# A graph layer on one core: GpSimd hands one of 64 row gathers to SyncE

## The chip, the cores and the metric

The kernel runs on 1 core of one Trainium2 chip. The metric is the device time of one execution in microseconds (us), as the median of several runs. The engines are TensorE (PE; its weight loads are shown apart, as PEld), VectorE (DVE), ScalarE (ACT), GpSimd (POOL) and SyncE (SP). Rows with a q (SPq, ACTq, DVEq) are work of an engine's own queue of instructions: waits, register work, the issue of transfers.

## The reference

One layer of message passing over N = 12500 nodes of 64 values and E = 200000 edges. `src` is random; `dst` is sorted and denser at low nodes. In short:

```
nodes   = x[[src, dst]]                        # E x 128
gates   = (ssp(edge_attr @ We1 + be1) @ We2 + be2) * cutoff(edge_weight)
h       = ssp(nodes @ Wn1 + bn1) @ Wn2 + bn2   # ssp(v) = softplus(v) - ln 2
sums    = zeros_like(x).at[dst].add(h * gates)
new     = x + ssp(sums @ Ws1 + bs1) @ Ws2 + bs2
return layernorm(x + new)
```

## The kernel before

The edges are taken in 391 **quads** of 512, in order of `dst`. A quad has two pairs of 256 edges; a pair's destinations lie in one range of W = 64 nodes, whose first node is in the table `w_all`. SP and DVE read it into registers (TENSOR_LOAD in the trace, L378 for SP and L1140 for DVE). For each quad:

- **POOL** (its `fast_step`) gathers the rows `x[src]` into `ga`, four indirect DMAs of 128 rows each (L459), into a ring of ARING = 16 quads. Before a quad it waits until PE has transposed the quad 15 earlier (`xe_t`).
- **SP** (its `fast_step`, one turn for two quads) reads four range starts (L378), waits on `oht_b` for DVE's pick of three quads before (L325), then issues `relb` (L326, the edges' places in their ranges), four `bw` (L335, one range's rows each of the table `b_tab`, which is x times the lower half of Wn1) and one `ea` (L318, the edge attributes of two quads). `ea` and `relb` have rings of 4 quads, `bw` one of 8. Between turns it stores shares of `b_tab` (L357) in the first quads, and finished nodes (L399) from quad 221 on, every 8 quads.
- **PE** in step s: `front(s)` (L623, L585) makes both hidden layers' inputs, where the second half of L623 multiplies `bw` by DVE's one-hot `ohT`; `transposes(s+2)` (L575 for `ea`, L577 for `ga`); `back(s-3)` (L653) sums messages over their ranges; `mid(s-1)` (L636, L640) is the second layers. `transposes` waits for `ea` and `ga` to have landed.
- **ACT** in step s: absolute values of `front(s)` (L852, L854), copy of the transposes (L844), exp (L860), a fill of PSUM with the bias (L871), log (L865).
- **DVE** in step s: `hidden(s-1)` (L1114, L1118), `message(s-2)`, `pick(s+2)` (L1100, `ohT` from `relb`), `one_hot(s-1)` (L1106), and `flush(s-3)` (L1152), which adds a range's sums to `acc` at an address from a register.

From step 206 on, every 8 steps one group of 500 nodes is finished beside the edges (L662, L671 on PE); three groups are left for the end. In steps 4 to 95 the shares of `b_tab` are made in the same way. Steps are written out or looped on each engine by hand; nothing plans them. There is a general path for other data; a flag chooses at run time and this data take the fast one. With sorted edges a pair's destinations must lie within W nodes for that.

Of the kernel before, what the change touches and what calls it, by code (L numbers as in the profile page):

```python
# [9 lines left out]
I32 = mybir.dt.int32  # L10
# [5 lines left out]
P = 128  # L16
PAIR = 2 * P
QUAD = 2 * PAIR
W = 64
# [5 lines left out]
BRING = 8  # L25
IN_RANGE = "windows' places are the least of N - W and of destinations, which are nodes"

# [29 lines left out]
def gnn_layer(nc, x, src, dst, edge_attr, dist, We1, be1, We2, be2, Wn1, bn1, Wn2, bn2,  # L57
# [29 lines left out]


# [20 lines left out]
    with ExitStack() as ctx:  # L109
# [10 lines left out]
        w_tab = nc.dram_tensor("w_tab", (1, RG * P * 2), I32, kind="Internal").ap()  # L120

# [63 lines left out]
        bw = sb("bw", [P, BRING, F])  # L185
        relb = sb("relb", [P, RING, PAIR], U8)
# [14 lines left out]
        dst_i = rows_d[:, :, :].rearrange("p g e -> p (g e)")[:, 0:NT].bitcast(I32)  # L201
        gen_flat = sb("gen_flat", [P, 10 * P])
# [58 lines left out]

        filled, hg_set = sem("filled"), sem("hg_set")
# [21 lines left out]
        def _(sp):  # L284
# [22 lines left out]
            def load_ea(q, u):  # L307

                if reached(q, RING):
                    sp.wait_ge(xe_t, q - (RING - 2))  # L310
                if isinstance(q, int) and q == NQ - 1:
                    full = edge_attr[q * QUAD:q * QUAD + PAIR, :].rearrange("(p j) d -> p (j d)", j=2)
                    sp.dma_start(ea[:, u, 0, :], full).then_inc(s_ea[u], 16)
                    part = edge_attr[q * QUAD + PAIR:E, :].rearrange("(p j) d -> p (j d)", j=2)
                    sp.dma_start(ea[0:REMP // 2, u, 1, :], part).then_inc(s_ea[u], 16)
                else:
                    two = edge_attr[bass.ds(q * QUAD, 2 * QUAD), :]
                    sp.dma_start(ea[:, u:u + 2, :, :].rearrange("p q k c -> p (q k) c"),  # L318
                                 two.rearrange("(m p j) d -> p m (j d)", p=P, j=2)).then_inc(s_ea[u], 16)

            def load_rel(q, u):

                if reached(q, RING):
# [1042 lines left out]
```

## Time and profile before

| what | value |
|---|---|
| median of 3 runs | 1991.15 us (1990.34 to 1991.43) |
| the profiled execution | 1991.78 us, of which the span of the profile is 1989.6 us |
| mean granted TensorE clock | 0.946 of full speed |
| busy, of the span | PE 88%, POOL 75%, ACT 74%, DVE 64% |
| chain that ended last | POOL 55%, "issue" 20%, PE 14% |
| DMA | 157.78 MB, 79 GB/s over the span |

How to read it: busy time is the time in which an engine had an instruction in it; "issue" is time in which an engine waited for nothing that the profile shows. The chain is followed back from the last instruction, at each step to what released it. Releasers are inferred. The profile covers one execution, and its durations are of that one.

### The profile page before, as it was taken

The page shows a single profiled execution, that of the slowest core. Times are in us where ns is not written, and L with a number is a line of the kernel's source. Part 1 is how long each engine was busy: PE and PEld are TensorE (multiplying, and loading weights), DVE is VectorE, ACT ScalarE, POOL GpSimd, SP SyncE. Part 2 cuts the span into 40 slices and gives each one's busy share as a digit, 9 for nine tenths or more (in the row PEclk, how much of TensorE's full clock was granted, in tenths as well). Part 3 has the DMA queues.
Part 4 walks back from the last instruction along what each step waited for, and adds up shares of the span by engine and source line. Part 5 has one row for each costly group of instructions (what it writes and reads, how often), then busy time and mean ns, then how long its engine had stood idle before and what let it go on. Part 6 is the DMA issues. An engine that isn't in the chain of part 4 may idle for free.

```text
span 1989.6 us, 52758 instructions
## 1 busy us (share of the span) xinstructions
PE 1744.9 (88%) x16249; PEld 1331.2 (67%) x16249; DVE 1281.8 (64%) x3512; ACT 1470.9 (74%) x2586; POOL 1483.8 (75%) x1572
## 2 busy tenths in 40 slices
PE   4699999989889888899888998888998898888897
PEld 3477777777667666666666776666776666666666
DVE  4577777766655655656566666666666666666666
ACT  2478888877776777767677777777777777777776
POOL 7777777777777777777777777777777777777773
PEclk7799999998998999989999999999989999999999
DMA  5433333333333333333333333333333333333331
GB/s 120 118 89 96 93 95 93 91 93 77 90 74 69 73 70 73 75 69 73 70 76 72 74 77 77 75 74 80 73 75 75 77 75 75 75 77 75 75 76 38
DMA packets 256432, 157.78 MB, mean 79 GB/s; under 512 B 45401, under 2 KB 227046, under 8 KB 256366
## 3 DMA queue, kind: packets, MB, share of 16 engines
q1 hardware_dynamic: 202652, 104.94, 18.1%
q0 software_dynamic: 50048, 51.35, 15.6%
q10 hardware_dynamic: 3666, 0.68, 0.2%
q8 instruction: 33, 0.54, 0.1%
q14 instruction: 33, 0.27, 0.1%
HBM read 146.94 MB, written 9.87 MB: 79 GB/s over the span
## 4 chain that ended last, share of the span: by engine, by line
POOL 55%; issue 20%; PE 14%; ACT 3%; DVE 2%; DMA 2%; SPq 2%; ACTq 1%; DVEq 0%; POOLq 0%
POOL ga L459 55%; PE ps L623 4%; PE ps L636 3%; PE ps L640 2%; PE ps L585 1%; PE ps L575 1%; DMA ga<-in_x_dram,srcT 1%; DVE hid L1114 1%; SPq L340 1%; ACT lg L865 1%; PE ps L653 1%; ACT lg L860 1%; PE ps L662 1%; PE ps L577 1%; DVE hid L1118 1%
## 5 line engine op out<-in xcount | busy, mean ns | idle before, releaser
L459 POOL DMA_INDIRECT ga<-in_x_dram,srcT x1564 | 1482.8, 948 | 477.7 <-issue 472.4
L852 ACT ACTIVATE lg<-ps,bn1c 128x512 f32<-128x512 f32 x391 | 268.6, 687 | 374.9 <-PE ps L585 351.7
L636 PE MATMUL ps<-wn,hid 128*128 128x64 f32 x3128 | 446.6, 287 | 35.7 <-DVE hid L1118 31.0
L1114 DVE SCALAR_TENSOR_TENSOR hid<-ps,neg_b,lg 128x512 f32<-128x512 f32 x391 | 293.0, 749 | 264.5 <-ACT lg L865 253.0
L636 PEld LDWEIGHTS ps<-wn,hid 128*128 128x128 f32 x3128 | 391.8, 197 | 71.6 <-DVE hid L1118 48.5
L860 ACT ACTIVATE lg<-lg 128x768 f32<-128x768 f32 x391 | 335.6, 858 | 0.0
L865 ACT ACTIVATE lg<-lg 128x768 f32<-128x768 f32 x391 | 332.2, 850 | 0.0
L575 PE MATMUL ps<-ident,ea 128*128 128x128 f32 x782 | 173.6, 305 | 174.2 <-DMA ga<-in_x_dram,srcT 117.6
L844 ACT COPY xe<-ps 128x512 f32<-128x512 f32 x391 | 230.0, 588 | 104.9 <-PE ps L577 92.0
L623 PE MATMUL ps<-xe,wn 64*128 64x256 f32 x1564 | 293.1, 453 | 0.0
L640 PE MATMUL ps<-we,hid 128*128 128x128 f32 x1564 | 274.5, 301 | 0.0
L1152 DVE TENSOR_TENSOR acc<-acc,ps 64x64 f32 x782 | 168.1, 215 | 160.7 <-issue 155.0
L575 PEld LDWEIGHTS ps<-ident,ea 128*128 128x128 f32 x782 | 80.1, 143 | 257.6 <-issue 242.0
L623 PE MATMUL ps<-ohT,bw 64*128 64x256 f32 x1564 | 249.6, 398 | 0.0
L1106 DVE TENSOR_TENSOR oh<-ps,relT 128x256 f32<-128x256 f32 x391 | 163.5, 418 | 114.6 <-PE ps L653 103.0
L871 ACT COPY ps<-bsum 128x512 f32<-128x512 f32 x391 | 234.9, 601 | 0.0
L640 PEld LDWEIGHTS ps<-we,hid 128*128 128x128 f32 x1564 | 218.8, 202 | 0.0
L1118 DVE SCALAR_TENSOR_TENSOR hid<-ps,neg_b,lg 128x256 f32<-128x256 f32 x391 | 185.9, 475 | 0.0
L854 ACT ACTIVATE lg<-ps,be1c 128x256 f32<-128x256 f32 x391 | 182.6, 467 | 0.0
L1100 DVE TENSOR_SCALAR ohT<-relb,iota_p 128x256 f32<-128x256 uint8 x391 | 149.2, 382 | 49.5 <-PE ps L585 42.3
L585 PE MATMUL ps<-xe,we 64*64 64x128 f32 x3128 | 180.9, 303 | 0.0
L653 PE MATMUL ps<-oh,msg 128*64 128x64 f32 x3128 | 179.9, 237 | 0.4 <-DVE msg L1133 0.3
(122 smaller groups left out, 1526.3 us busy)
## 6 DMA issues: line engine op xcount, KB each, us to landing
ea<-in_edge_attr_dram SPq DMA_DIRECT2D x195, 256.0 KB
ga<-in_x_dram,srcT POOLq DMA_INDIRECT x1564
bw<-b_tab SPq DMA_DIRECT2D x782, 32.0 KB
relb<-rel_tab SPq DMA_DIRECT2D x196, 64.0 KB
b_tab<-share SPq DMA_DIRECT2D x25, 250.0 KB
out_dram<-xs SPq DMA_DIRECT2D x25, 125.0 KB
xs<-in_x_dram SPq DMA_DIRECT2D x3, 750.0 KB
rows_i<-in_dst_dram SPq DMA_DIRECT2D x1, 768.0 KB
```

Source lines behind the costliest of these rows:

```text
L459: pool.indirect_dma_start(to[:, t % 2, t // 2, :], None, x, bass.IndirectOffsetOnAxis(ap=idx[:, t:t + 1], axis=0)).then_inc(done, 16)
L575: pe.transpose(ps_xe[:, k * P:(k + 1) * P], ea[:, u, k, :], ident[:, :])
L623: pe.matmul(ps[:, 2 * (u % 2) + k, 0:PAIR], weights, rows, start=(end == 0), stop=(end == 1), skip_group_check=True)
L636: pe.matmul(hg[:, t * D:(t + 1) * D], hid[:, u % 2, t * P:(t + 1) * P], wn2[:, :], start=False, stop=False, skip_group_check=True)
L640: mm = pe.matmul(gates[:, :, j, :], hid[:, u % 2, QUAD + j * P:QUAD + (j + 1) * P], we2[:, :].rearrange("p (k d) -> p k d", k=2), start=Fa ...
L844: act.copy(xe[:, u, :, :].rearrange("p h e -> p (h e)"), ps_xe[:, :]).then_inc(xe_e, 1)
L852: act.activation(lg[:, u % 2, 0:QUAD].rearrange("p (k e) -> p k e", k=2), z[:, :, 0:PAIR], ACT.Abs, bias=bn1c[:, 0:1])
L860: act.activation(lg[:, u % 2, :], lg[:, u % 2, :], ACT.Exp, scale=-1.0).then_inc(z_exp, 1)
L865: act.activation(lg[:, u % 2, :], lg[:, u % 2, :], ACT.Ln, bias=1.0).then_inc(z_ln, 1)
L871: act.copy(hg, bsum[:, :, :, :].rearrange("p h k d -> p (h k d)")).then_inc(filled, 1)
L1114: dve.scalar_tensor_tensor(out=hid[:, u % 2, 0:QUAD].rearrange("p (k e) -> p k e", k=2), in0=ps[:, 2 * (u % 2):2 * (u % 2) + 2, 0:PAIR], s ...
L1118: dve.scalar_tensor_tensor(out=hid[:, u % 2, QUAD:QUAD + PAIR].rearrange("p (j e) -> p j e", j=2), in0=ps[:, 2 * (u % 2):2 * (u % 2) + 2, ...
```

## The change

Four things are changed together.

1. **Rows by SP.** For 20 quads (80, 96, ... 384: `ROW_QUADS`), POOL issues three gathers instead of four; the 128 rows of the fourth are fetched by SP, each by a DMA of one row of 256 B into a buffer `stage` of two slots, at a byte address that SP reads into a register. The 128 are spread over eight turns of SP (16 rows a turn, `ROWS_TURN`), from 22 quads before the quad (`ROWS_BEFORE`) on. So SP has 16 rows in every turn from quad 58 to quad 376. Four quads before the quad, `hand_rows` waits for the rows and copies `stage` to `ga` by one DMA, which counts up `handed`; PE waits on `handed` at every 8th quad. The addresses (`row_at`, 2560 of them, picked from `src` at every second element) are loaded once by SP and scaled once by DVE.
2. **Ranges of 46 nodes.** W is 46; `bw` loads 46 rows, and PE, DVE work on 46 nodes where they had 64. The halves stay at partitions 0 and 64 (`HALF`).
3. **Range starts in bytes.** A second table `wb_tab`/`wb_all` holds them times 512; SP reads eight at once, every second turn. SP's loops are written out in full.
4. **ACT issues `ea`**, after the log of every odd step, for the quads 5 and 6 later.

```diff
-W = 64
+HALF = 64
+W = 46
+ROWS0, ROWS_EVERY, ROWS_N, ROWS_BEFORE, ROWS_TURN, HAND = 80, 16, 20, 22, (16,) * 8, 8
 # SyncE
 def load_bw(q, v, firsts):
     if reached(q, BRING):
         sp.wait_ge(z_mm, q - (BRING - 2))
     for n, first in enumerate(firsts):
-        sp.dma_start(bw[n % 2 * W:(n % 2 + 1) * W, v + n // 2, :],
-                     b_tab[bass.ds(first, W), :]).then_inc(s_bw[v], 16)
+        sp.dma_start(bw[n % 2 * HALF:n % 2 * HALF + W, v + n // 2, :].bitcast(U8),
+                     b_bytes[bass.ds(first, W * F * 4)].rearrange("(r b) -> r b", b=F * 4)).then_inc(s_bw[v], 16)
+def load_rows(q):
+    i, turn = divmod(q - (ROWS0 - ROWS_BEFORE), ROWS_EVERY)
+    turn //= 2
+    ...
+    if i >= 2 and turn == 0:
+        sp.wait_ge(xe_t, ROW_QUADS[i - 2] + 1)
+    first, n = ROWS_FIRST[turn], ROWS_TURN[turn]
+    _, places = nc.values_load_multi_w_load_instructions(
+        row_at[:, i * P + first:i * P + first + n], engines=(mybir.EngineType.SP,), ...)
+    for r, place in enumerate(places):
+        sp.dma_start(stage[first + r:first + r + 1, i % 2, :].bitcast(U8),
+                     x_bytes[bass.ds(place, D * 4)].rearrange("(r b) -> r b", r=1)).then_inc(s_stage[i % 2], 16)
+def hand_rows(q):
+    i, off = divmod(q - (ROWS0 - 4), ROWS_EVERY)
+    if 0 <= i < ROWS_N and off == 0:
+        quad = ROW_QUADS[i]
+        sp.wait_ge(s_stage[i % 2], P * 16 * (i // 2 + 1))
+        sp.wait_ge(xe_t, quad - (ARING - 1))
+        sp.dma_start(ga[:, quad % ARING, 1, 1, :], stage[:, i % 2, :]).then_inc(handed, 16)
+    if q > ROWS0 and q % HAND == 0 and q not in ROW_QUADS:
+        sp.sem_inc(handed, 16)
 def fast_step(q, v):
-    _, firsts = nc.values_load_multi_w_load_instructions(w_all[0:1, bass.ds(q * 2, 2 * n)], ...)
+    if v % 4 == 0:
+        _, starts[0:2 * m] = nc.values_load_multi_w_load_instructions(wb_all[0:1, bass.ds(q * 2, 2 * m)], ...)
     load_rel(q, u)
     load_bw(q, v, firsts)
-    if reached(q, RING):
-        load_ea(q, u)
+    load_rows(q)
+    hand_rows(q)
 # before the first turn
+sp.wait_ge(row_e, XCOLS)
+sp.dma_start(row_at..., src[...][:, :, (ROWS_EVERY - 1) * QUAD + PAIR + 1:ROWS_EVERY * QUAD:2]).then_inc(ld_row, 16)
 # GpSimd, fast_step
+if q in ROW_QUADS:
+    gather(to, idx, 0, done)
+    gather(to, idx, 1, done)
+    gather(to, idx, 2, done, 32)
+else:
+    gather_rows(to, idx, done)
 # TensorE
 def transposes(q, v):
     pe.wait_ge(s_ga[v], per_ring(q, v, ARING, 64))
+    if v % HAND == 0 and reached(q, ARING):
+        pe.wait_ge(handed, q * (16 // HAND) - (16 // HAND * ARING - 16))
 def front(q, v, node=None, share_off=None):
-    ... (bw[half, b, :], ohT[half, u % 2, :])
+    near = slice(k * HALF, k * HALF + W)
+    ... (bw[near, b, :], ohT[near, u % 2, :])
 # ScalarE, fast_step
     logs(q, u)
+    if u % 2 == 1:
+        load_ea(q + RING + 1, (u + 1) % RING)
 # VectorE, once, after step 7
+dve.wait_ge(ld_row, 16)
+dve.tensor_scalar(row_at, row_at, float(D * 4), None, ALU.mult).then_inc(row_ready, 1)
```

## Rows read from the trace of the kernel before

**Rows 1.** The page: its head, busy times, and the chain that ended last.

```profile
span 1989.6 us, 52758 instructions
PE 1744.9 (88%) x16249; PEld 1331.2 (67%) x16249; DVE 1281.8 (64%) x3512; ACT 1470.9 (74%) x2586; POOL 1483.8 (75%) x1572
...
POOL 55%; issue 20%; PE 14%; ACT 3%; DVE 2%; DMA 2%; SPq 2%; ACTq 1%; DVEq 0%; POOLq 0%
```

**Rows 2.** The gathers: the whole span, then its end (ns: least, median, most).

```profile
L459 POOL DMA_INDIRECT ga<-in_x_dram,srcT x1564: 940/944/2408, 3.1 to 1961.3; - x196
...
L459 POOL DMA_INDIRECT ga<-in_x_dram,srcT x1531: 940/944/2408, 3.1 to 1920.0; - x192
```

**Rows 3.** Waits: POOL's in the whole span, then PE's from 400 to 1900 us.

```profile
POOL ga L459 <- issue: 472.4, 1550, 0.3
POOL ga L459 <- PE ps L577: 4.0, 13, 0.3
...
PE ps L575 <- DMA ga<-in_x_dram,srcT: 113.5, 127, 2.1
...
PEld ps L575 <- issue: 210.3, 293, 2.3
PEld ps L575 <- DMA ga<-in_x_dram,srcT: 9.5, 7, 2.2
```

**Rows 4.** The chain from 1915 to 1926 us (start, us, what).

```profile
1920.01 0.95 POOL ga L459
1920.96 0.30 issue
1921.26 2.98 DMA ga<-in_x_dram,srcT
1924.24 0.23 issue
1924.47 0.43 PE ps L575 x2
```

**Rows 5.** SP's own waits, 307 to 1891 us.

```profile
SPq L325 <- DVE ohT L1100: 738.3, 160, 10.3
```

**Rows 6.** SP in order of time, 1309 to 1314 us: one turn.

```profile
1309.77 0.65 SPq L326 DMA_DIRECT2D relb<-rel_tab  x1
1310.71 2.50 SPq L335 DMA_DIRECT2D bw<-b_tab  x4
1313.42 0.44 SPq L318 DMA_DIRECT2D ea<-in_edge_attr_dram  x1
```

**Rows 7.** Turns: the `relb` issues up to 307 us and up to 1891 us.

```profile
L326 SPq DMA_DIRECT2D relb<-rel_tab x30: 607/627/5223, 36.6 to 306.7; - x30
...
L326 SPq DMA_DIRECT2D relb<-rel_tab x190: 607/622/5223, 36.6 to 1890.7; - x190
```

**Rows 8.** SP in its first 12 us; L289 is a DMA of one row.

```profile
2.26 0.43 SPq L287 DMA_DIRECT2D rows_i<-in_dst_dram  x1
2.73 0.24 SPq L289 DMA_DIRECT2D rows_i<-in_dst_dram  x1
3.02 0.76 SPq L291 DMA_DIRECT2D rows_i<-in_dst_dram  x1
...
10.48 0.50 SPq L289 DMA_DIRECT2D rows_i<-in_src_dram  x1
11.02 0.61 SPq L291 DMA_DIRECT2D rows_i<-in_src_dram  x1
```

**Rows 9.** Register reads (SP four, DVE eight), then DVE's last two (two, six).

```profile
L378 SPq TENSOR_LOAD <-w_all x196: 332/477/1981, 36.2 to 1946.5; - x196
L1140 DVEq TENSOR_LOAD <-w_all x116: 519/1844/2161, 77.8 to 1970.9; - x116
...
L1140 DVEq TENSOR_LOAD <-w_all x2: 524/680/837, 1970.0 to 1970.9; - x2
```

**Rows 10.** SP's `bw` issues, and its stores from 125 partitions.

```profile
L335 SPq DMA_DIRECT2D bw<-b_tab x782: 468/469/2946, 37.5 to 1951.5; - x196
...
L399 SPq DMA_DIRECT2D out_dram<-xs x25: 271/341/410, 1108.8 to 1986.5; - x25
```

**Rows 11.** ACT: four issues in its first 9 us; its waits, 400 to 1900 us.

```profile
6.30 2.49 ACTq L784 DMA_DIRECT2D wn<-in_L_gnn_Wn_dram  x4
...
ACT lg L852 <- PE ps L585: 286.0, 261, 5.6
```

**Rows 12.** DMA queues: packets, MB, share of 16 engines.

```profile
q1 hardware_dynamic: 202652, 104.94, 18.1%
```

**Rows 13.** Steps by ACT's L852, 100 to 340 us; then two stretches: busy us, clock, DMA share.

```profile
L852 ACT ACTIVATE lg<-ps,bn1c x55: 687/688/691, 104.8 to 338.7; 128x512 f32<-128x512 f32 x55
...
300.00:400.00 100.00, 96.84 (x984) 75.77 (x984) 78.11 (x213) 84.87 (x151) 75.62 (x81) 1.00 0.38 94
400.00:1100.00 700.00, 611.16 (x5652) 465.20 (x5651) 429.27 (x1159) 504.27 (x856) 529.36 (x561) 0.93 0.33 75
```

**Rows 14.** DMA issues: KB each, us to landing.

```profile
w_tab<-w_i ACTq DMA_DIRECT2D x1, 4.0 KB, 6.9
```

More of the change, by code:

```diff
@@ L25 @@
 BRING = 8
+ROWS0 = 80
+ROWS_EVERY = 16
+ROWS_N = 20
+ROWS_BEFORE = 22
+ROWS_TURN = (16,) * 8
+HAND = 8
+ROWS_FIRST = tuple(sum(ROWS_TURN[:n]) for n in range(len(ROWS_TURN)))
 IN_RANGE = "windows' places are the least of N - W and of destinations, which are nodes"
+IN_X = "sources are nodes"
 def reached(i, n):
@@ L85, in gnn_layer @@
     assert RG > 1 and RL > 1
+    ROW_QUADS = [ROWS0 + ROWS_EVERY * i for i in range(ROWS_N)]
+    assert sum(ROWS_TURN) == P and all(n % 4 == 0 for n in ROWS_TURN) and 2 * len(ROWS_TURN) == ROWS_EVERY
+    assert ROWS0 % HAND == 0 and ROWS_EVERY % HAND == 0 and ROWS0 >= ROWS_EVERY and ROW_QUADS[-1] < NQ - 4
     STEPS = 8
@@ L260, in gnn_layer @@
         g_oh, g_mm, g_add = ([sem(f"{n}{k}") for k in range(2)] for n in ("g_oh", "g_mm", "g_add"))
+        ld_row, row_ready, wb_ready, wb_stored = (sem(n) for n in ("ld_row", "row_ready", "wb_ready", "wb_stored"))
+        handed = sem("handed")
+        s_stage = [sem(f"s_stage{k}") for k in range(2)]
         filled, hg_set = sem("filled"), sem("hg_set")
@@ L278, in general_of, with issue_ea @@
             return eng.value_load(flag_i[0:1, 0:1], min_val=0, max_val=1)
+        def issue_ea(eng, q, u):
+            if isinstance(q, int) and q == NQ - 1:
+                full = edge_attr[q * QUAD:q * QUAD + PAIR, :].rearrange("(p j) d -> p (j d)", j=2)
+                eng.dma_start(ea[:, u, 0, :], full).then_inc(s_ea[u], 16)
+                part = edge_attr[q * QUAD + PAIR:E, :].rearrange("(p j) d -> p (j d)", j=2)
+                eng.dma_start(ea[0:REMP // 2, u, 1, :], part).then_inc(s_ea[u], 16)
+            else:
+                two = edge_attr[bass.ds(q * QUAD, 2 * QUAD), :]
+                eng.dma_start(ea[:, u:u + 2, :, :].rearrange("p q k c -> p (q k) c"),
+                              two.rearrange("(m p j) d -> p m (j d)", p=P, j=2)).then_inc(s_ea[u], 16)
         N_DST = 4
@@ L310, in load_ea @@
                     sp.wait_ge(xe_t, q - (RING - 2))
[L311 to L319, printed above, removed]
+                issue_ea(sp, q, u)
             def load_rel(q, u):
@@ L621, in front @@
                         half = slice(k * D, (k + 1) * D)
-                        weights, rows = (wn1[half, 0, :], xe[half, u, 1, :]) if end == 0 else (bw[half, b, :], ohT[half, u % 2, :])
+                        near = slice(k * HALF, k * HALF + W)
+                        weights, rows = (wn1[half, 0, :], xe[half, u, 1, :]) if end == 0 else (bw[near, b, :], ohT[near, u % 2, :])
                         pe.matmul(ps[:, 2 * (u % 2) + k, 0:PAIR], weights, rows,
```

87 lines of the change are left out of this document (54 added, 33 removed).

## The prediction

> **What bounds the kernel now.** I read the page first. TensorE is the busiest engine, but the chain that ended last is GpSimd's for 55% of the span, and a further 20% is called "issue" [rows 1]. What that issue is, the gathers' own row tells: 1564 of them start between 3.1 and 1961.3 us, so one every (1961.3 - 3.1)/1563 = 1.253 us, of which 0.944 is the instruction and the rest the gap behind it [rows 2]. The waits say that the gap is GpSimd's own: 1550 waits on "issue", and 13 of 0.3 us each on TensorE, no longer than the gap itself [rows 3]. GpSimd thus never stops from the first gather to the last. One quad costs it 5.01 us, whatever the rest does.
>
> TensorE starts late and catches up. Between 104.8 and 338.7 us it makes 55 steps, 4.33 us each, with TensorE 97% busy at the full granted clock; behind 400 us it is 87% busy [rows 13] and waits for gathers: its loads before L575 sit idle for 210 + 10 us between 400 and 1900 us, in some 300 quads, so 0.73 us a quad [rows 3]. So from about quad 75 on a gather is what each step waits for. The chain leaves GpSimd for good at the landing of the gather that starts at 1921.26 [rows 4], which is number 1532, the last of quad 382 [rows 2]. What follows, 68 us of TensorE, ScalarE and DVE for the last steps and nodes, stays.
>
> **What the change takes from the bound.** Of the 20 quads with three gathers, 19 (80 to 368) lie before that point. Each saves one period: 19 x 1.253 = 23.8 us. The twentieth, quad 384, is bounded by 0 and 1.3; I take 0, since the chain has left GpSimd there. TensorE has to run 1.25 us faster in 16 quads and has 16 x 0.73 = 11.7 spare, so it follows. The increment of 32 on the third gather I cost at nothing (bounds 0 and one gap, 0.31 x 20 = 6 us).
>
> **ScalarE's loads.** Some 194 issues of 128 partitions each, one in 2 quads. The same engine's static issues took 2.49/4 = 0.62 us [rows 11], SyncE's for `ea` 0.44 [rows 6]. They come between the log and the absolute values of the next step, for which ScalarE waits 286 us in 261 cases, 1.1 us a time [rows 11]. That idle time hides them; without it they would cost 0.62/2 = 0.3 us a quad, still under the 0.73 spare. Before 340 us there is less cover, and TensorE would catch up some quads later, which costs the end nothing. The wait on `xe_t` inside is one that the copy of the transposes, earlier in the same step, has already made.
>
> **46 nodes, DVE and TensorE.** Fewer columns in L653, L1106, L1152 make work off the path shorter (0 to 1 us at the end, in the last nine steps); I take 0. The scaling of `row_at`, 2560 elements on one partition, stands in DVE's queue once; the steps behind it wait some us, in the stretch in which TensorE is late anyway, and GpSimd's 16 quads of ring cover it.
>
> **The start.** SyncE has one more wait and a transfer of 2560 pieces of 4 B ahead of its first turn. The nearest row is `w_tab`, 512 pieces in 6.9 us [rows 14]; five times as many give up to 34 us, and down to 1 if pieces overlap. `ea` for quads 6 and on no longer stands behind the 19 us in which SyncE loads `xs`. GpSimd needs the first transposes only at 3.1 + 64 x 1.253 = 83 us. I take 0 for the end, with up to 20 as the bound. The second table goes the way of the first beside it.
>
> **SyncE, where it is decided.** It gets 16 register values and 16 transfers in every turn from quad 58 to quad 376. If a turn takes longer than two quads of the others, `relb` comes late, then `ohT`, then TensorE's `front`, and SyncE's period becomes that of the kernel. In the stretch from the 30th `relb` (quad 58, 306.7 us) to the 190th (quad 378, 1890.7) a turn is (1890.7 - 306.7)/160 = 9.90 us [rows 7], of which SyncE waits 738.3/160 = 4.61 [rows 5] and works 5.29. With 23.8 us less in the same 160 turns the period is 9.75. So up to a turn of T = 9.75 us the gain is whole, at 9.90 it is gone, and the time is
>
> 1967.4 + 160 x (T - 9.75) above that.
>
> The new turn, item by item. `relb`: 0.65 and a wait, 0.7 [rows 6]. Four `bw`: in the trace 0.47 us each [rows 10] in a period of about 0.65; a store from 125 partitions takes 0.34 [rows 10]. Issues differ by their shape and not by bytes, and 46 rows have not been seen; I take 0.34 + 0.11 between = 0.45 each, 1.8, with 1.5 (the least store, 0.27) and 2.6 (as before) for bounds. Register reads: four values in 0.477, six in 0.837, so a further four or part of four 0.36; eight every second turn, 0.42, and sixteen 0.48 + 3 x 0.36 = 1.56, bounds 0.48 and, as below, 3.7 [rows 9]. The hand-over, the node stores and the waits, a few issues per eight turns: 0.3. Without the rows that is 4.8.
>
> The rows: a DMA of one row was issued three times, shown are 0.24 us (2.73 to the next start at 3.02, a period of 0.28) and 0.50 (a period of 0.54, behind transfers that had filled the queue) [rows 8]. From quad 58 on the DMA queues are a third busy [rows 13], so I take the free case, 0.28: 16 x 0.28 = 4.5, bounds 16 x 0.24 = 3.8 and 16 x 0.54 = 8.6. The register work for a dynamic address, some 0.18 us between two `bw`, I count into the period: ScalarE's issues of 64 partitions stand at 0.62 + 0.03 without it, SyncE's at 0.47 + 0.18 with it, so the period is one and the same [rows 6, 10, 11]. The sum is T = 4.8 + 4.5 = 9.3 us, 0.45 under the limit. The lower bounds give 0.7 + 1.5 + 0.4 + 0.5 + 0.3 + 3.8 = 7.2, the upper ones 0.7 + 2.6 + 0.9 + 3.7 + 0.3 + 8.6 = 16.8.
>
> **The sum.** 1989.6 - 23.8 = 1965.8 us of span; the profiled execution took 2.2 more than its span, 1968.0, and the median is 0.6 below the profiled time: 1967.4.
>
> **A rule against it.** For the registers the rows give 0.12 us a value in fours and 0.23 in the eight of DVE [rows 9]. The Trainium skill (Runtime: NRT & Kernel Launch, "Instruction fetch mechanics") says that a TENSOR_LOAD costs about 200 ns a register even in bulk. SyncE's four in 0.477 disagree, DVE's eight in 1.844 agree. By that rule, an estimate, the turn would be 9.3 - 1.98 + 3.2 + 0.8 = 11.3 us and the kernel 2219.
>
> **The rivals.**
>
> *The row issues are the new bound* (slower, 0.24). The place is SyncE's sixteen DMAs in a turn; the price is their period p. The gain is whole up to p = (9.75 - 4.8)/16 = 0.309, and above (9.90 - 4.8)/16 = 0.319 the kernel is slower. For it: register work of about 0.1 us beside 0.24 would give 0.34, T = 10.24 and 2046 us; and two of the three one-row issues took twice 0.24. Against: these two stood in a full queue. At p = 0.54 it would be T = 13.4 and 2551.
>
> *The registers come in pairs or singly* (slower, 0.08). DVE's eight took 1.844 us, 0.23 a value [rows 9]. For sixteen 3.7, for eight 1.84/2: T = 9.3 - 1.98 + 3.7 + 0.9 = 11.9, and 2311 us. Against: SyncE's four took no longer than one or two, and its new reads start, like those, at multiples of four values; DVE's start at odd quads.
>
> *SyncE just binds* (faster by less, 0.10): T between 9.75 and 9.88, 1972 to 1987. A turn with a node store or a hand-over is longer than the mean and the rings take only some of it.
>
> *No change* (0.06): the same within 4 us, by T near 9.9, or by a start that stalls GpSimd for the 20 us of its bound.
>
> *The transfers crowd on few DMA engines* (slower, 0.02). A packet takes 0.181 x 16 x 1989.6/202652 = 28 ns [rows 12]. If the 4 x 46 rows and the 16 of a turn went through two of 16 engines, these would have 92 + 16 packets, 3.0 us, on top of a third of 9.8; 6.3 of 9.8 us, still enough, but gathers land up to 3 us later. Since GpSimd does not wait for landings, that shifts the end by up to 3 us once; it only decides if bursts delay `relb` (period over 9.9). By the Trainium skill (DMA: Bandwidth & Descriptors, "Why a DMA increments its semaphore by 16 and not by 1") the number of engines is the largest up to 16 that divides the slowest dimension, so two for 46 rows and one for a row; no row here shows the engine.
>
> **How the numbers follow.** A measurement here tells 0.2%, 4 us, from no change. Whole gain: 0.50, 1963 to 1972 (its own range). With the partial one: faster 0.60. Same 0.06. Slower 0.24 + 0.08 + 0.02 = 0.34. Of that, T up to 10.4, p up to 0.35, holds 0.15 and reaches 2075 us; what is above, some 0.19, is left out. The range is 1963 to 2075.
>
> **What would show it.** Right: 1544 gathers at the same 1.25 us period, the last at about 1936; SyncE's wait on DVE's L1100 down to some 0.5 us a turn but not gone; a row's issue every 0.28 us; the read of sixteen at 1.6 us; PE's wait at L575 still for gathers. Wrong: no wait left at L325, DVE waiting for `relb` before L1100, GpSimd waiting for TensorE (`xe_t`), TensorE before L623 idle and its granted clock down. The forecast falls first with the issue price of one row, then with the read of sixteen registers.

## The result, and the profile after

| kernel | median, us | executions | clock of the profiled execution |
|---|---|---|---|
| before | 1991.29 | 1990.34 to 1991.83 | 0.946 |
| changed | 2045.37 | 2039.12 to 2061.47 | 0.871 |

The ratio is 1.0284 [1.0261, 1.0307], so the changed kernel is 54 us slower. The forecast was 1967.4 us and faster; the time lies inside the range, near the time of the first rival (2046). The ratios here and below, with their 95% intervals in brackets, leave out executions that fell in the chip's second, slower state: two of the ten of e5c, and three of the six of the last kernel on the second chip of the last table. The profiled execution of the changed kernel is the slowest of its four, 2061.47 us, and has the lowest granted clock (the others 0.878 to 0.891).

The page says at once that another engine sets the time. In [rows 1] the chain was GpSimd's for 55%; GpSimd is no longer in it:

```profile
span 2059.7 us, 56246 instructions
PE 1859.5 (90%) x16249; PEld 1423.7 (69%) x16249; DVE 1234.9 (60%) x3514; ACT 1463.2 (71%) x2586; POOL 1465.7 (71%) x1552
...
SPq 39%; PE 34%; issue 12%; ACT 8%; DVE 4%; DMA 2%; ACTq 1%; DVEq 1%
```

The waits of all engines, and then SP's own from 307 to 1900 us (engine, line, tile, who ended the wait; us in all, times, longest):

```profile
POOL ga L508 <- issue: 458.0, 1502, 0.3
...
PE ps L638 <- SPq L395: 70.8, 19, 7.6
...
DVE ohT L1180 <- DMA relb<-rel_tab: 42.4, 18, 11.3
...
POOL ga L508 <- PE ps L640: 35.1, 41, 3.6
```

```profile
SPq L354 <- DVE ohT L1180: 72.0, 22, 6.3
SPq L364 <- PE ps L648: 2.5, 7, 0.6
```

SP waited 738.3 us in 160 turns [rows 5]; between the 30th turn and the 190th (quads 58 to 378) it now waits 65.9 us, 0.41 a turn. The forecast took 0.5 for a sign that it was right, but as a mean it misleads: the wait falls in some 20 turns only, and 45.2 us of it behind 1452 us, where TensorE was slow (below). TensorE's waits for gathers [rows 3] are gone: between 400 and 1900 us there is none. In their place it waits for the hand-over that SP signals (L395), DVE waits for `relb`, and GpSimd waits for TensorE up to 3.6 us at a time, since its ring of 16 quads is full. DVE's wait for `relb`, GpSimd's for TensorE and the lower clock are signs that the forecast named as its refutation.

SP's instructions by line (ns: least, median, most; start of the first and of the last):

```profile
L382 SPq MOVE stage<-in_x_dram x2560: 29/29/38, 327.9 to 1962.8; - x197
L382 SPq DMA_DIRECT2D stage<-in_x_dram x2560: 224/228/647, 328.0 to 1962.8; - x197
...
L378 SPq TENSOR_LOAD <-rows_i x160: 1152/1232/1408, 326.7 to 1956.6; - x160
...
L364 SPq DMA_DIRECT2D bw<-b_tab x782: 235/254/4367, 40.7 to 2021.0; - x196
...
L441 SPq TENSOR_LOAD <-wb_all x98: 702/787/2367, 38.0 to 2004.2; - x98
...
L508 POOL DMA_INDIRECT ga<-in_x_dram,srcT x1544: 938/944/2124, 3.0 to 1959.9; - x193
```

And two turns in order of time (start, us, what; a group of several spans its gaps):

```profile
1305.42 0.55 SPq L355 DMA_DIRECT2D relb<-rel_tab  x1
1306.08 1.42 SPq L364 DMA_DIRECT2D bw<-b_tab  x4
1308.86 5.09 SPq L382 DMA_DIRECT2D stage<-in_x_dram  x16
1314.05 0.54 SPq L392 DMA_DIRECT2D ga<-stage  x1
1314.65 0.47 SPq L463 DMA_DIRECT2D out_dram<-xs  x1
1315.24 0.54 SPq L355 DMA_DIRECT2D relb<-rel_tab  x1
1315.89 2.97 SPq L364 DMA_DIRECT2D bw<-b_tab  x4
1320.26 5.09 SPq L382 DMA_DIRECT2D stage<-in_x_dram  x16
1326.29 0.56 SPq L355 DMA_DIRECT2D relb<-rel_tab  x1
```

A row costs 0.228 us of issue, but sixteen take 5.09 from the first start to the last end, so one starts every (5.09 - 0.23)/15 = 0.324 us. The register work for its address (a MOVE of 0.029 and gaps) stands beside the issue and not inside it. The first turn lasts 1315.24 - 1305.42 = 9.82 us, with no wait in it. In the second one `bw` issue stalls: the four take 2.97 us where they took 1.42, and the turn is 11.05.

**Where the time went.** SP's turns are numbered; the 30th belongs to quad 58, where the rows begin. The start of the `relb` issue of four of them, in us, from the profiled execution of each kernel (those after the first two rows are the experiments of the next section):

| kernel | 30th (quad 58) | 54th (106) | 142nd (282) | 190th (378) |
|---|---|---|---|---|
| before | 306.7 | 532.8 | 1411.8 | 1890.7 |
| changed | 324.3 | 580.6 | 1452.2 | 1963.3 |
| e1, no rows | 315.8 | 532.7 | 1425.9 | 1901.7 |
| e2, every 32nd quad | 309.0 | 536.0 | 1403.8 | 1881.6 |
| e3, every 24th quad | 310.3 | 532.6 | 1401.1 | 1876.7 |
| e4, table later | 318.0 | 575.6 | 1437.8 | 1911.3 |
| e5c, rows from 128 | 318.2 | 540.9 | 1418.6 | 1892.1 |
| e9, every 24th, W 64 | 307.1 | 531.4 | 1400.9 | 1878.3 |
| e10, every 16th, W 64 | 308.2 | 581.9 | 1514.3 | 2028.2 |

The changed kernel is 17.6 us late at the 30th turn, loses 30.2 more in the next 24 turns (10.68 us each against 9.42), gains 7.4 back in the following 88 (9.90 against 9.99), and loses 32.2 in the last 48 (10.65 against 9.98). Together that is 72.6, and the profiled times differ by 69.7.

**The middle loss: turns 30 to 54.** SP does not wait for DVE or TensorE once between its 30th turn and its 54th, so the 10.68 us of a turn are all its own. They are 1.0 us more than its work in the next 88 turns, 9.67. In this stretch SP stores a share of `b_tab` in every second turn, and the read of eight range starts stands right behind that store. The read takes much longer there (from 324 to 581 us, then from 581 to 1452 us):

```profile
L441 SPq TENSOR_LOAD <-wb_all x12: 1620/2081/2367, 334.2 to 568.5; - x12
L441 SPq TENSOR_LOAD <-wb_all x44: 702/785/954, 589.4 to 1442.0; - x44
```

That is 1.3 us in two turns, or 0.65 a turn; the issue of the store (0.28 us and a gap in two turns) adds 0.17, and slower `bw` issues 0.19. With sixteen rows a turn the read takes as long in e4 (2.06 us) and e10 (2.13), without rows 1.05 (e1) and 1.07 (e5c); why it is slow is not shown. The kernel before has the same stores there and waits to cover them.

**The last loss: turns 142 to 190** goes with the granted clock: of its 511.1 us SP waited 45.2, and its work, 9.71 us a turn, is below the 9.98 of the kernel before. **The first loss, ahead of the 30th turn,** is the clock's in part. The stretches of the changed kernel (busy us of PE, PEld, DVE, ACT, POOL; then clock, DMA share, GB/s):

```profile
115.00:130.00 15.00, 15.00 (x88) 11.43 (x86) 8.06 (x20) 7.38 (x13) 11.36 (x12) 0.50 0.26 45
130.00:145.00 15.00, 15.00 (x105) 11.08 (x104) 7.85 (x22) 7.62 (x14) 11.33 (x12) 0.63 0.32 75
324.00:581.00 257.00, 227.49 (x2052) 176.25 (x2050) 161.99 (x451) 178.63 (x313) 194.51 (x206) 0.87 0.41 80
581.00:1452.00 871.00, 803.43 (x7154) 613.34 (x7152) 515.83 (x1483) 643.07 (x1121) 658.61 (x697) 0.89 0.37 72
1452.00:1963.00 511.00, 479.01 (x3984) 365.11 (x3984) 296.60 (x864) 364.43 (x660) 367.74 (x389) 0.84 0.34 69
1460.00:1475.00 15.00, 15.00 (x84) 11.24 (x83) 6.06 (x17) 6.76 (x13) 11.34 (x13) 0.50 0.35 65
1475.00:1490.00 15.00, 15.00 (x84) 11.07 (x82) 6.40 (x18) 7.89 (x14) 11.34 (x13) 0.50 0.24 55
```

In the 15 us from 1460 and from 1475 TensorE is busy all the time and runs at 0.50 of full speed, the lower of its two levels, 1.2 GHz. Its steps then take 7.4 us (five of ACT's L921 between 1466.5 and 1496.2). After 1452 us there are three such stretches of some 50 us, from 1452, 1619 and 1790. One of 31 us, from 110 us, lies ahead of the 30th turn. The steps there (ACT's L921, up to 107 and up to 150 us):

```profile
L921 ACT ACTIVATE lg<-ps,bn1c x8: 687/687/703, 60.1 to 106.7; 128x512 f32<-128x512 f32 x8
L921 ACT ACTIVATE lg<-ps,bn1c x14: 687/687/703, 60.1 to 149.0; 128x512 f32<-128x512 f32 x14
```

The eighth step starts at 106.7 us, 1.9 after that of the kernel before, and the fourteenth at 149.0, 18.3 after: six steps in 42.3 us, 7.05 each, where the kernel before made one in 4.33 [rows 13]. The first of the six took 11.0 us. In it DVE waited 5.0 us for the `relb` that SP issued at 94.17 us, 11.5 later than before, and TensorE was busy for 7.4. SP's turns were late from the start: its first four `bw` issues, behind the transfer of 2560 addresses, took 10.21 us (2.94 before, 1.43 in e4, an experiment of the next section, where that transfer comes later; in this order before, changed, e4):

```profile
37.51 2.94 SPq L335 DMA_DIRECT2D bw<-b_tab  x4
40.72 10.21 SPq L364 DMA_DIRECT2D bw<-b_tab  x4
37.66 1.43 SPq L364 DMA_DIRECT2D bw<-b_tab  x4
```

In e1, which has the same transfer ahead of its turns, this step is as long (10.9 us), with the same wait, and the five behind it take the usual time. So by this comparison some 9 us of the 17.6 go with SP's late turns, and some 9, most of it in the next five steps, with the low clock.

### The profile page after: what moved, and what is told of

Read it like the earlier page. It is cut to its first block, busy times and chain, and to the rows that moved or that the text cites. A ratio compares the mean times of both kernels' runs of the same rounds, so it can differ in the third digit from the quotient of the medians.

```text
span 2059.7 us, 56246 instructions
## 1 busy us (share of the span) xinstructions
PE 1859.5 (90%) x16249; PEld 1423.7 (69%) x16249; DVE 1234.9 (60%) x3514; ACT 1463.2 (71%) x2586; POOL 1465.7 (71%) x1552
## 3 DMA queue, kind: packets, MB, share of 16 engines
q0 software_dynamic: 49408, 50.69, 18.4%
## 4 chain that ended last, share of the span: by engine, by line
SPq 39%; PE 34%; issue 12%; ACT 8%; DVE 4%; DMA 2%; ACTq 1%; DVEq 1%
SPq L382 19%; PE ps L687 9%; PE ps L700 9%; SPq L364 8%; SPq L378 6%; PE ps L704 4%; PE ps L648 3%; PE ps L638 2%; SPq L355 2%; SPq L441 2%; PE ps L717 2%; ACT lg L934 2%; ACT lg L929 2%; DVE hid L1194 2%; PE ps L640 2%
## 5 line engine op out<-in xcount | busy, mean ns | idle before, releaser
L508 POOL DMA_INDIRECT ga<-in_x_dram,srcT x1544 | 1464.7, 949 | 494.4 <-issue 458.0
L921 ACT ACTIVATE lg<-ps,bn1c 128x512 f32<-128x512 f32 x391 | 268.7, 687 | 468.0 <-PE ps L648 448.8
L700 PE MATMUL ps<-wn,hid 128*128 128x64 f32 x3128 | 483.6, 303 | 59.7 <-DVE hid L1198 55.4
L700 PEld LDWEIGHTS ps<-wn,hid 128*128 128x128 f32 x3128 | 427.1, 212 | 95.4 <-DVE hid L1198 77.6
L704 PE MATMUL ps<-we,hid 128*128 128x128 f32 x1564 | 290.5, 313 | 0.0
L687 PE MATMUL ps<-ohT,bw 46*128 46x256 f32 x1564 | 264.7, 418 | 0.0
L1232 DVE TENSOR_TENSOR acc<-acc,ps 64x46 f32 x782 | 153.7, 197 | 171.7 <-issue 165.5
L1186 DVE TENSOR_TENSOR oh<-ps,relT 128x184 f32<-128x184 f32 x391 | 134.0, 343 | 149.2 <-PE ps L717 141.6
L717 PEld LDWEIGHTS ps<-oh,msg 128*64 128x64 f32 x3128 | 134.6, 148 | 90.9 <-issue 86.5
L717 PE MATMUL ps<-oh,msg 128*64 128x46 f32 x3128 | 184.0, 252 | 14.8 <-DVE acc L1232 14.3
L687 PEld LDWEIGHTS ps<-ohT,bw 46*128 46x128 f32 x1564 | 170.9, 212 | 25.6
```

The costliest lines, as they stand in the source:

```text
L508: pool.indirect_dma_start(to[:, t % 2, t // 2, :], None, x, bass.IndirectOffsetOnAxis(ap=idx[:, t:t + 1], axis=0)).then_inc(done, inc)
L687: pe.matmul(ps[:, 2 * (u % 2) + k, 0:PAIR], weights, rows, start=(end == 0), stop=(end == 1), skip_group_check=True)
L700: pe.matmul(hg[:, t * D:(t + 1) * D], hid[:, u % 2, t * P:(t + 1) * P], wn2[:, :], start=False, stop=False, skip_group_check=True)
L704: mm = pe.matmul(gates[:, :, j, :], hid[:, u % 2, QUAD + j * P:QUAD + (j + 1) * P], we2[:, :].rearrange("p (k d) -> p k d", k=2), start=Fa ...
L717: mm = pe.matmul(sums[k * D:(k + 1) * D, 0:W], msg[:, u % 2, 2 * k + j, :], oh[:, u, 2 * k + j, :], start=(j == 0), stop=(j == 1))
L921: act.activation(lg[:, u % 2, 0:QUAD].rearrange("p (k e) -> p k e", k=2), z[:, :, 0:PAIR], ACT.Abs, bias=bn1c[:, 0:1])
```

## The experiments

The experiments ran on two chips, e7d and e10 on one and the others on the other; the kernel before took between 1990.96 and 1991.66 us beside them, as beside the changed kernel. Runs on two further chips are told of at the end.

**e1: SyncE fetches no rows; all else as changed.** It separates the rows from the other parts.

```
 def load_rows(q):
+    return
 # hand_rows: no hand-over, only its signal; POOL: always gather_rows(to, idx, done)
```

> The changed kernel without its rows by SyncE: GpSimd gathers all four groups of every quad, nothing is handed over; the ranges of 46, the byte table, the written-out loops, the attribute loads on ScalarE, TensorE's waits and the table load at the start stay. Theory A (SyncE's turn is the bound, 9.63 us of work in it, of which the rows and their register read are 6.6): the turn has 3.0 us of work, SyncE waits again, GpSimd sets the end, and the late start is caught up: 1991 us, within 4, and SyncE's wait on VectorE near 6 us a turn. Theory B (the rest of the change costs the time: the start, few-engine transfers of 46 rows, ScalarE's issues): above 2000 us.

**e2 and e3: fewer rows in a turn.** Rows for every 32nd quad (eight a turn, 10 quads), or every 24th (12, 12 and 8, 13 quads).

```
-ROWS_EVERY, ROWS_N, ROWS_BEFORE, ROWS_TURN = 16, 20, 22, (16,) * 8
+ROWS_EVERY, ROWS_N, ROWS_BEFORE, ROWS_TURN = 32, 10, 38, (8,) * 16           # e2
+ROWS_EVERY, ROWS_N, ROWS_BEFORE, ROWS_TURN = 24, 13, 30, (12, 12, 8) * 4     # e3
```

> A row group for every 32nd quad instead of every 16th, 8 rows in a turn instead of 16, 10 groups in all. A: work of a turn 9.63 - 8 x 0.335 - 0.4 = 6.5 us, SyncE not bound, ten gathers less on GpSimd: 1991.3 - 12.5 = 1979 us (1976 to 1982). B: half of the slowdown or more stays, above 2010 us.

> A row group for every 24th quad, 12, 12 and 8 rows in a turn, 13 groups. A: work of a turn 9.63 - 5.3 x 0.335 - 0.3 = 7.5 us on average and 8.0 in the longer ones, still under 9.75: 1991.3 - 13 x 1.253 = 1975 us (1972 to 1979). B: above 2010 us.

| kernel | median (executions), us | ratio to before |
|---|---|---|
| e1 | 2000.42 (1997.83 to 2005.37) | 1.0051 [1.0033, 1.0069] |
| e2 | 1987.63 (1984.73 to 2000.04) | 0.9992 [0.9974, 1.0009] |
| e3 | 1982.73 (1978.64 to 1983.30) | 0.9955 [0.9938, 0.9972] |

Without the rows 45 of the 54 us are gone; with two thirds of them per turn all is gone and the kernel is 9 us faster than before, clear of its interval. All three miss the time that was expected if SP's turn is the bound (1987 to 1995, 1976 to 1982, 1972 to 1979), by 5 us, 6 and 4. e2 and e3 are far from the 2010 of the other theory; e1 stands at its edge (2000), so the rest of the change costs some 9 us of its own, which e6c to e7d look into. The page of e3 (head and chain), its gathers, and SP's waits from 307 to 1900 us say why:

```profile
span 1976.8 us, 54450 instructions
...
POOL 35%; PE 26%; issue 17%; ACT 8%; DMA 5%; DVE 5%; ACTq 2%; DVEq 1%; SPq 0%; POOLq 0%
```

```profile
L508 POOL DMA_INDIRECT ga<-in_x_dram,srcT x1551: 940/944/1960, 3.0 to 1945.1; - x194
```

```profile
SPq L354 <- DVE ohT L1180: 334.8, 109, 12.7
```

The last gather starts 16.2 us earlier than before [rows 2], and 13 gathers fewer at 1.253 are 16.3: GpSimd's gain is there, in full, once SP waits again. Of it the median shows 8.6. In e2 the last gather starts at 1949.5, 11.8 us earlier for 10 gathers fewer, and the median shows 3.7, no change by its interval. Part of the rest comes behind the last gather (31.7 us in e3's profile, 28.3 before), and e3's profiled execution is the shortest of its four; it was not followed further.

The waits also give the work of a turn: what lies between the 30th and the 190th less SP's waits there, divided by 160. It is 9.83 us in the changed kernel ((1639.0 - 65.9)/160), 7.79 in e3, 6.82 in e2 and 3.21 in e1. So a row costs (9.83 - 3.21)/16 = 0.414 us with its share of the register read, and (7.79 - 3.21)/10.67 = 0.43 in e3; the two agree.

**e10: the changed kernel with ranges of 64.** On SP only the `bw` issues are meant to grow: 0.545 us each for 64 rows where 46 take 0.254. If the turn is the bound, the kernel must be slower by what this adds, and GpSimd's work is the same.

```
-W = 46
+W = 64
```

> The changed kernel whole, with ranges of 64 instead of 46: nothing but the price of the four bw issues in SyncE's turn goes up, from 0.25 to 0.54 us or a little less each, 0.9 us a turn. A (the turn is the bound): 160 turns x 0.9 = 144 us more, less what the few-engine transfers give back: 2045 + 100 to 144, so 2145 to 2190 us. If SyncE's turn is not the bound, ranges of 64 make it faster, as they do without the rows (1995 against 2000): 2040 or less.

2124.16 us (2123.72 to 2137.72), 1.0687 [1.0650, 1.0725]; 79 us over the changed kernel, which is far above the 2040 of a kernel that SP's turn does not bound, and 21 below the least that was expected. The work of a turn grew by 0.87 us, from 9.83 to 10.70, as expected (0.9). But the turn itself grew only from 10.24 to 10.75, since SP's waits went from 65.9 us to 7.3. So in the changed kernel SP was not the only bound: part of the added work took the place of waits. In the profiled executions the 160 turns add 81 us, and e10 was 16 us less late at the 30th, which leaves 65; their times differ by 62. The chain of e10:

```profile
SPq 50%; PE 22%; issue 13%; ACT 5%; DVE 4%; DMA 3%; ACTq 1%; DVEq 1%
```

**e4: the table of row addresses loaded later**, just ahead of SP's turn of quad 16 and no longer ahead of its first; DVE scales it 16 steps later.

```
-sp.dma_start(row_at..., src[...])          # before the first turn
+if q == 2 * BRING:                         # in the turn of quad 16
+    sp.dma_start(row_at..., src[...])
```

> Only the load of the 2560 addresses is moved, from ahead of SyncE's first turn to quad 16 (and VectorE's scaling with it, to after step 23). Sixteen rows a turn stay. A: the turn stays the bound from quad 58 on, so what the start loses is never caught up; the 18 us by which TensorE was late at step 20 fall to under 5, and the median falls by some 14 us, to about 2031 (2024 to 2038). If the start does not matter, 2045 as before.

2015.95 us (2009.21 to 2023.75), 1.0123 [1.0088, 1.0157]: 29 us under the changed kernel, and below the 2024 to 2038 that were expected. The table says where. At the 15th turn it is 1.6 us late where the changed kernel is 18.0, as expected; then it loses 10 over a stretch of 21 us at the low clock (0.51, from 183 us), and is 11.3 late at the 30th (the changed kernel 17.6). It loses about what the changed kernel does in the next 24 turns (31.5), and then does better than before for 136, 9.82 us each against 9.98: between the 142nd turn and the 190th no low stretch of it is longer than 24 us, and the mean clock is 0.93 where the changed kernel has 0.84. These last 48 turns are 38 of the 52 us between the two kernels at the 190th turn; what moved the clock is open.

What the transfer costs at the start varies. At the fifth turn e4 is 0.3 us late, and the profiled executions with the transfer ahead are 1.0 (e9) to 13.7 (e5c) late, the changed kernel 11.5, e1 12.2, e2 2.7, e3 6.4 and e10 4.5; at the 30th it is 0.4 in e9 and 17.6 in the changed kernel. They differ up to there in the number of addresses (1280 in e2, 1664 in e3 and e9, 2176 in e5c, else 2560), in the ranges, and in that e2 and e3 start their rows earlier (quads 42 and 50), so the numbers are no clean comparison.

e4 also shows that GpSimd no longer sets the end: its last gather starts at 1938.7 us, near the forecast's 1936, and the kernel still ends at 2013.7.

**e5c: the rows start at quad 128**, so that sixteen rows a turn begin at quad 106, behind the stretch in which TensorE catches up.

```
-ROWS0, ROWS_N = 80, 20
+ROWS0, ROWS_N = 128, 17
```

> The same kernel as in e5_rows_from_128, with its expectations, on a chip where the kernel before takes 1991 us (the sessions of e5 to e8 ran on two chips where it took 2508): 1972 to 1985 us if the stretch of the shares' stores is what cost the time, above 2010 if sixteen rows a turn are too many anywhere.

2003.91 us (1984.60 to 2042.51, ten executions), 1.0045 [1.0014, 1.0075]; without the two longest (2022.74 and 2042.51) the median is 2001.5. With the same sixteen rows in every later turn, 41 to 44 of the 54 us are gone; the spread is wide. The 24 turns from the 30th, now without rows, take 9.28 us each, not 10.68. The median lies between the two expectations (1972 to 1985, above 2010) and meets neither: the stretch of the shares' stores is the larger part, and sixteen rows a turn are still too many behind it for a gain.

**e6c, e8c, e7d: what e1 has left.** e1 is 9 us over before although it fetches no row. These are e1 with ranges of 64, with ranges of 48, and with `ea` loaded by SyncE again.

```
-W = 46
+W = 64     # e6c;  48 in e8c
 # e7d, SyncE: if reached(q, RING): load_ea(q, u); ScalarE's loads left out
```

> As for e6_no_rows_w64, against the 2000 us and the clock of 0.906 of e1_no_rows: C (narrow ranges lower TensorE's granted clock) and D (46 rows on few DMA engines) 1991 us and a clock near 0.945; F (ScalarE's issues) 2000.

> As for e8_no_rows_w48: C about 2000 us and a clock near 0.91; D 1991 us and a clock near 0.94. On the other two chips the clock was 0.76 with 48 and 0.83 with 64, which speaks for C.

> As for e7_no_rows_ea_sp, against the 2000 us of e1_no_rows. Ranges of 64 and of 48 gave 1995 and 1996, so some 5 us are D's (few-engine transfers) and 3 to 4 us are left. F (ScalarE's issues of the edge attributes): 1996, a gain of 3 to 4. D alone: 2000, within 3, or later by a little since the attribute loads then queue behind the 46-row transfers.

| kernel | median (executions), us | ratio to before | chain: POOL, PE | low stretches |
|---|---|---|---|---|
| e1 (46) | 2000.42 (1997.83 to 2005.37) | 1.0051 [1.0033, 1.0069] | 29%, 31% | 11 |
| e7d (46) | 1997.26 (1994.80 to 2004.96) | 1.0030 [1.0019, 1.0041] | 31%, 30% | 12 |
| e8c (48) | 1995.87 (1993.55 to 2006.78) | 1.0024 [1.0009, 1.0039] | 31%, 30% | 9 |
| e6c (64) | 1994.77 (1992.84 to 1997.18) | 1.0014 [1.0004, 1.0024] | 54%, 13% | 1 |

The last column counts, of the hundred stretches of 15 us from 400 to 1900 us, those with a granted clock under 0.62. The kernel before has 1, the changed one 20. Ranges of 64 bring the profile of before back (chain and clock), and 6 of the 9 us; no kernel gets back to 1991, which C and D forecast for 64. e8c is as fast with the clock still low. So the clock is not what most of the 9 us pays for. The intervals of e1 and e7d overlap; ScalarE's loads cost 3 us or nothing. Those of e1 and e8c overlap as well, so the 4.6 us between 46 and 48 rows are a sign and not a proof.

What changes between 46 rows and 48, by the DMA queues' rows (packets, MB, share of 16 engines; e1, then e8c; q0 has GpSimd's gathers, q1 SP's transfers):

```profile
q0 software_dynamic: 50048, 51.35, 19.1%
q1 hardware_dynamic: 78102, 47.01, 8.8%
q0 software_dynamic: 50048, 51.35, 14.4%
q1 hardware_dynamic: 90614, 47.86, 8.9%
```

There are 782 `bw` transfers. With 48 rows each has (90614 - 78102)/782 = 16 packets more, and only 2 of them are rows; with 64 (e6c, 103126) each has 32 more, and 18 are rows. The other 14 are there in both, as if a transfer of 46 rows ended on two engines and one of 48 or 64 on sixteen. And the same gathers' packets take a third more of the DMA engines' time beside 46 rows: 19.1% in e1 and e7d, 14.4% with 48, 14.7% with 64. So theory D's crowding is seen. It did not lengthen TensorE's waits for gathers from 400 to 1900 us (63.4 us in e1, 64.5 in e8c), and what it costs in time, up to the 4.6 us, is not shown.

**e9: e3 with ranges of 64.** The best of both.

```
-W = 46
+W = 64
-ROWS_EVERY, ROWS_N, ROWS_BEFORE, ROWS_TURN = 16, 20, 22, (16,) * 8
+ROWS_EVERY, ROWS_N, ROWS_BEFORE, ROWS_TURN = 24, 13, 30, (12, 12, 8) * 4
```

> A row group for every 24th quad as in e3 (1983 us) and ranges of 64 as before. A with C or D: the turn is 7.5 + 1.0 us, still under 9.75, the 8 us that e3 lacked to its forecast come back: 1975 us (1972 to 1979), clock 0.94. If the ranges of 46 were needed to make room in the turn, 1990 or more.

1982.79 us (1975.67 to 1984.80), 0.9938 [0.9915, 0.9962]. The clock came back (0.936 in the profile, and none of the hundred stretches is low), the 8 us did not: the median is above the 1979 that was expected and no faster than e3. At 10.7 rows a turn GpSimd has the largest share of the chain in both (48% in e9), and TensorE's speed is spare. e3 and e9 are faster than the kernel before, by 0.5% and 0.6%, and than the changed one.

**e5, e6, e7, e8 and their repeats, on two other chips.** There the kernel before itself takes 2508.08 and 2509.29 us.

> The changed kernel with its first row quad at 128 instead of 80 (17 groups instead of 20; SyncE's first rows come at quad 106, behind the shares' stores), sixteen rows a turn as before. Theory A, refined: from quad 58 to 104 SyncE also waits for the shares' stores, its turn is 10.7 us there, and TensorE, which would catch up, loses 29 us (quad 60 to 105: 243 us against 214); behind 105 the turn takes 9.8. Then this kernel loses only the small part behind 105: 16 gathers before quad 382, 1991.3 - 20 = 1971 if the turn fits, and 1972 to 1985 since it hardly does. If the sixteen rows are too many anywhere, above 2010.

> The kernel without rows by SyncE (2000 us, clock 0.906) with ranges of 64 again. Three theories for its 9 us over the kernel before. C (narrow ranges give TensorE narrower work, and its granted clock falls): 1991 us and a clock near 0.945. D (46 rows travel on few DMA engines, so gathers land late in bursts): 1991 us too, clock up. F (ScalarE's issues of the edge attributes): stays at 2000.

> The kernel without rows by SyncE (2000 us), ranges of 46, the edge attributes issued by SyncE again as in the kernel before. F: back to 1991 us. C and D: stays at 2000, within 4.

> The kernel without rows by SyncE with ranges of 48 instead of 46. The work of TensorE and VectorE is 4% wider there, no more. C: about 2000 us and a clock near 0.91, as with 46. D (48 rows can be dealt out to 16 engines evenly, 46 can't): 1991 us, the clock at 0.94, and a bw issue of some 0.47 us as with 64 rows instead of 0.25. F: 2000.

> The same kernel as in e5_rows_from_128, with the same expectations (A, refined: 1972 to 1985 us; above 2010 if sixteen rows a turn are too many anywhere), beside a kernel before that takes its usual 1991 us; in the session of e5 to e8 the kernel before itself took 2508.

> As for e6_no_rows_w64: C (narrow ranges lower TensorE's granted clock) and D (46 rows on few DMA engines) 1991 us and a clock near 0.945; F (ScalarE's issues) 2000.

> As for e7_no_rows_ea_sp: F (ScalarE's issues of the edge attributes) 1991 us; C and D stay at 2000, within 4.

> As for e8_no_rows_w48: C about 2000 us and a clock near 0.91; D 1991 us, clock 0.94, a bw issue of some 0.47 us instead of 0.25; F 2000.

| kernel | first chip, us (ratio) | second chip, us (ratio) |
|---|---|---|
| rows from 128 | 2609.66 (1.0395 [1.0360, 1.0430]) | 2600.57 (1.0373 [1.0345, 1.0402]) |
| no rows, 64 | 2524.51 (1.0060 [1.0038, 1.0083]) | 2528.33 (1.0072 [1.0051, 1.0093]) |
| no rows, 48 | 2531.35 (1.0095 [1.0062, 1.0128]) | 2545.48 (1.0113 [1.0074, 1.0152]) |
| no rows, `ea` by SyncE | 2577.56 (1.0290 [1.0258, 1.0322]) | 2578.12 (1.0188 [1.0149, 1.0227]) |

The bound is another one there, so these do not answer the question; e5c, e6c, e8c and e7d are the same kernels on the chips of the others. In the profile of the 64-node kernel on the first of them, a gather takes 949 ns and an exp of ACT 862, as in e6c (949 and 861), but GpSimd stands idle for 941.2 us before gathers (477.6 in e6c), the largest part of it on a releaser that the profile does not resolve:

```profile
POOL ga L509 <- remote: 413.7, 283, 2.3
POOL ga L509 <- issue: 363.4, 1192, 0.3
POOL ga L509 <- PE ps L641: 162.9, 88, 20.5
```

What this shows is that GpSimd is not the bound of this kernel there, so that taking gathers from it is not expected to pay. By their medians ranges of 48 are some 0.3% to 0.7% slower than those of 64 there, with overlapping intervals, and those of 46 (with `ea` by SyncE) more; on the first chip the clock of the profiled execution was 0.828 with 64, 0.762 with 48 and 0.753 with 46.

## Why the prediction was wrong

Two steps failed. The price of a row's issue was 0.28 us in the sum T = 9.3 and measured 0.324, which takes the turn's work to 9.83, over the limit of 9.75. And the step from T to a time failed: the forecast compared one mean turn with one mean limit, by which 9.83 would give 1980 us, and 2045 was measured.

**What bounds the kernel before** was right: the chain, and e3, where 13 gathers less moved the last one by 16.2 us. The gain of 23.8 for 19 gathers was not seen in the changed kernel; its last gather started at 1959.9 and not at 1936, because GpSimd had to wait for TensorE. In e4 it started at 1938.7, and the kernel was still 25 us slower than before.

**The turn, T = 9.3 us, limit 9.75.** The mean work of a turn was 9.83. The part without rows and their read was put at 4.8 - 1.56 = 3.24 and measured 3.21 (e1). The rows with their read were put at 4.5 + 1.56 = 6.06 and measured 6.62. In it the read of sixteen was cheaper than said (1.23 us for 1.56, and eight 0.79 for 0.84), and so the row is what failed. The forecast took 0.28, the period of a static one-row issue, and counted the register work for a dynamic address into it, by a comparison with ScalarE's static issues of another shape. The measured period is 0.324: the issue, 0.228, and then the register work, a MOVE and gaps. That is the mechanism of the first rival, 0.34 in its words. The other two prices held: four `bw` took 1.47 us in the median, 1.76 in the mean and up to 4.1 with a stall (forecast 1.8), `relb` 0.55.

**By the forecast's own formula** the work of 9.83 would cost 160 x 0.08 = 13 us, and the miss is 78. The larger mistake was therefore to hold one mean against one limit over 160 turns. Three things break that.

- *Quads 58 to 104.* The forecast had TensorE catching up only until about quad 75, and put no price on the shares of `b_tab` that SP stores in these turns. Its work was 256.3/24 = 10.68 us, without a wait for another engine, and before a turn took 9.42 here. That costs 30 us in the changed kernel, 31.5 in e4; moving the rows behind the stretch (e5c) avoids it.
- *No slack.* A stall of SP (four `bw` issues of up to 4.1 us, a hand-over with a node store) or of TensorE (a low-clock stretch) is made good only if the turn is well under the limit. Before it had 4.61 us of waiting in a turn; now 0.41. GpSimd's ring of 16 quads did not help, as it was GpSimd that ran ahead.
- *The clock.* The forecast named a lower clock as a sign and gave it no price. The low stretches go with some 9 of the 17.6 us ahead of the 30th turn and with the 32 us of the last 48 turns in the profiled execution, where steps took up to 7.4 us and SP waited 45.2. No run holds the clock and changes nothing else, so this part is read from the trace and not isolated. The other three executions, at slightly higher clocks, are 13 to 22 us shorter.

With waits and all, the turn was 10.24 us, for which the formula gives 1967.4 + 160 x 0.49 = 2046; with the 17.6 at the start, which the formula lacks, it is 2063, near the 2061 of that execution. The first rival's 10.24 and 2046 are met by luck in part: its row price was near, but the turn that it put at 10.24 by work alone was 9.83 of work and 0.41 of waits, and its 2046 had no late start.

**The start** was costed at 0, bound 20. In e1 the late start is made up by the 54th turn (9.1 us late at the 30th, then none), so where SP has slack 0 was right. Where SP's turn is the bound it is not made up, and the changed kernel was 17.6 us late, some 9 with SP's late first turns and some 9 with the clock.

**ScalarE's loads** 0: in the changed kernel an issue takes 0.379 us, and e7d against e1 gives 3 us or nothing. **Ranges of 46** 0: without rows they cost 6 us (e1 against e6c). With rows the narrower ranges are worth 79 us (e10), because they shorten SP's turn; the forecast had that in its 1.8 for `bw`, with 2.6 as the upper bound.

**The other rivals.** Registers singly or in pairs: refuted, 1.232/16 = 0.077 us a value. The Trainium skill (Runtime: NRT & Kernel Launch, "Instruction fetch mechanics") says about 200 ns a register; the trace disagrees for reads by SP. Crowding on few DMA engines: it happens. The packets of the queues fit two engines for 46 rows, as the forecast said, and the gathers' packets take a third more engine time; but without rows by SP it costs some 5 us or less by the medians of 46 and 48 rows, and it is not what made the kernel slow, since e10 with 64 rows is slower still.

**Open**: what starts a stretch at the low clock, how large the clock's part of the 54 us is in the median (as against the profiled execution), and why e4's clock was higher, and so most of its 29 us.

## What to carry to other kernels

Work that is given to an idle engine has to fit its turn in every stretch, not on average: compare the new turn with the pace of the others stretch by stretch, with all that the engine does there, and keep some of the waiting (here 11 rows a turn paid, 16 did not). Price an issue by the distance between the starts of two, with the address work that a dynamic one needs. When a queue's waits fall near zero, each later stall goes straight into the time.

## What the runs showed of the hardware

- A read of sixteen consecutive values into SP's registers took 1.232 us, eight 0.787, four 0.477 [rows 9]: 0.077 a value in the longest. DVE's eight at odd quads took 1.844.
- SP's read of eight values right behind the issue of a share's store took 2.08 us (changed kernel, 324 to 581 us), elsewhere 0.785.
- The issue of a `bw` transfer on SP took 0.254 us (median) for 46 rows, 0.372 for 48 (e8c) and 0.542 for 64 (e6c; 0.469 in the kernel before, which addresses rows and not bytes); one row took 0.228, and sixteen started every 0.324.
- Each `bw` transfer of 48 or 64 rows has 14 packets more, beside its rows, than one of 46. With 46 rows the gathers' packets took 18.4% to 19.4% of the DMA engines' time (changed, e1 to e4, e5c, e7d), with 48 or 64 rows in byte addresses 13.8% to 14.7% (e6c, e8c, e9, e10).
- TensorE's clock fell to 0.50 for up to some 50 us, and TensorE was busy all the time in the stretch from 1452 to 1503 us. With ranges of 46 or 48 nodes 9 to 12 of 100 stretches of 15 us were low where GpSimd has the most of the chain or near it (e1, e2, e3, e7d, e8c), with 64 none or one (before, e6c, e9). With rows for every 16th quad it was 8 with 64 (e10), and with 46 it was 20 in the changed kernel and 11 in e4. So narrower ranges go with it in these single profiles, and so may the waits of a kernel that SP bounds; neither was isolated further.
- The kernel before took 1991 us on two chips and 2508 and 2509 on two others. For the 64-node kernel without rows, profiled on both kinds, gathers and exps lasted the same, TensorE's L701 307 ns on the slower chip and 291 on the other (clock 0.828 and 0.930), and GpSimd stood idle for 941 us and 478.
